# Products of the C rows and the states of a selective scan, in instructions of four states

## What is computed

```python
delta = softplus(einsum('er,brl->bel', dt_proj_w, dt_lo) + dt_proj_b)
A = -exp(A_log)                              # 512 channels x 16 states
def step(state, xs):
    d_t, B_t, C_t, u_t = xs
    dA = exp(d_t[..., None] * A)
    state = state * dA + (d_t * u_t)[..., None] * B_t[:, None, :]
    y_t = einsum('ben,bn->be', state, C_t)   # sum over the 16 states
    return state, y_t
y = (y + D * u) * silu(z)
```

## Time and profile before

| | us |
|---|---|
| median of 3 runs | 556.17 |
| lowest, highest | 554.56, 556.52 |
| the profiled execution | 554.37 |
| its span on the core | 552.6 |
| mean granted clock of PE, of full speed | 0.978 |

### The profile page before, as it was taken

How to read it: one execution, slowest core, us unless ns; L and a number is a source line. 1 busy time by engine, 2 the same in 40 slices (tenths; PEclk the granted TensorE clock), 3 DMA queues, 4 the chain that set the end, 5 groups by cost and what they waited for, 6 DMA issues and landing times.

```text
span 552.6 us, 9388 instructions
## 1 busy us (share of the span) xinstructions
PE 502.3 (91%) x3154; PEld 381.2 (69%) x3154; DVE 459.9 (83%) x844; ACT 395.3 (72%) x704; POOL 479.3 (87%) x359
## 2 busy tenths in 40 slices
PE   6668989898798899999999999999899999999788
PEld 2156979767677687759687887678667756676654
DVE  2878999969899989779899999787878878977952
ACT  3369687758776787577968787578789778777632
POOL 0169999999999999989999999989999999988920
PEclk9877999999989999999999999999999999999899
DMA  4793000127320001046220000066100000000001
GB/s 109 258 351 142 2 2 0 39 54 240 131 77 2 0 1 58 0 159 211 77 95 2 20 1 21 6 226 222 49 20 1 21 20 21 1 20 21 0 21 38
DMA packets 18274, 37.82 MB, mean 68 GB/s; under 512 B 5537, under 2 KB 6305, under 8 KB 18226
## 3 DMA queue, kind: packets, MB, share of 16 engines
q1 hardware_dynamic: 18226, 37.22, 20.3%
HBM read 32.75 MB, written 4.46 MB: 67 GB/s over the span
## 4 chain that ended last, share of the span: by engine, by line
PE 52%; POOL 15%; ACT 13%; DVE 10%; issue 8%; DMA 1%; DVEq 0%; ACTq 0%; SPq 0%; POOLq 0%
PE p_s L718 14%; PE p_y L740 12%; POOL state L541 8%; PE p_v L773 5%; PE p_f L764 5%; DVE state L1197 4%; POOL dbu L526 4%; PE p_tr L684 4%; ACT da L960 3%; PE p_pr L647 3%; DVE x L1145 2%; PE p_pr L640 2%; ACT p_s L960 2%; ACT L912 2%; ACT L960 1%
## 5 line engine op out<-in xcount | busy, mean ns | idle before, releaser
L541 POOL TENSOR_TENSOR state<-state,c_bc 128x1024 f32<-128x1024 f32 (+1 forms) x158 | 304.5, 1940 | 14.0 <-DVE state L1197 11.2
L1197 DVE TENSOR_TENSOR_SCAN state<-da,p_s 128x512 f32<-128x512 f32 (+1 forms) x158 | 172.7, 1104 | 28.7 <-PE p_s L718 27.3
L718 PEld LDWEIGHTS p_s<-pair_b,du_t 128*128 128x128 f32 x1264 | 163.9, 196 | 36.1 <-issue 22.6
L718 PE MATMUL p_s<-pair_b,du_t 128*128 128x128 f32 x1264 | 178.9, 283 | 4.0 <-DVE state L1197 2.5
L740 PE MATMUL p_y<-ident,state 128*128 128x128 f32 x1024 | 150.4, 275 | 0.8 <-POOL state L541 0.8
L960 ACT ACTIVATE da<-delta,a_neg 128x512 f32<-128x512 f32 (+1 forms) x190 | 119.2, 642 | 25.2 <-DVE state L1197 24.7
L740 PEld LDWEIGHTS p_y<-ident,state 128*128 128x128 f32 x1024 | 120.6, 142 | 20.2 <-issue 15.3
L526 POOL TENSOR_TENSOR dbu<-du,pair_b 128x1024 f32<-128x1024 f32 (+1 forms) x64 | 116.5, 1820 | 4.7 <-DMA pair_b<-bc_rows 4.7
L1197 DVE TENSOR_TENSOR_SCAN state<-p_s,dbu 128x512 f32<-128x512 f32 (+1 forms) x98 | 101.1, 1037 | 5.5 <-POOL dbu L526 4.5
L960 ACT ACTIVATE p_s<-delta,a_neg 128x512 f32<-128x512 f32 (+1 forms) x130 | 74.9, 580 | 39.4 <-DVE state L1197 38.7
L764 PE MATMUL p_f<-u_sb,h_t 128*128 128x512 f32 x112 | 55.2, 595 | 1.5 <-DVE gw L1298 1.5
(11 more groups left out here) (178 smaller groups left out, 612.9 us busy)
## 6 DMA issues: line engine op xcount, KB each, us to landing
c_bc<-bc_rows SPq DMA_DIRECT2D x32, 512.0 KB, 5.6
pair_b<-bc_rows SPq DMA_DIRECT2D x13, 512.0 KB, 6.4
xs<-in_x SPq DMA_DIRECT2D x16, 256.0 KB, 4.3
out<-ot SPq DMA_DIRECT2D x14, 256.0 KB, 2.0
cx<-in_ctx_t SPq DMA_DIRECT2D x4, 512.0 KB, 3.6
u_sb<-in_u_w SPq DMA_DIRECT2D x1, 1024.0 KB, 7.9
v_sb<-in_v_w SPq DMA_DIRECT2D x1, 1024.0 KB, 14.6
w_in<-in_in_w_t SPq DMA_DIRECT2D x1, 384.0 KB, 4.5
```

The source lines that it names most:

```text
L541: eng.tensor_tensor(pair, pair, c_bc[:, 2 * p:2 * p + 2, c0:c0 + w], ALU.mult).then_inc(po_cs, 1)
L718: mm = eng.matmul(p_s[g % BANKS][:, t * P:(t + 1) * P], du_t[:, f % 2, t, :], diagonals_of(n // 2)[:, n % 2, c0 // P + t, :], start=(t == ...
L1197: eng.tensor_tensor_scan(slot(g)[:, 0:w], decayed, added, first, ALU.mult, ALU.add).then_inc(ve_scan, 1)
```

## The change

In f = 12 to 18 POOL multiplies two pairs, four states, in one instruction, and in f = 12 to 15 copies the last columns of the four states in one. The groups are the pairs 0 and 1, 2 and 3, 4 and 5, 6 and 7; each is done at the place of its second pair and waits for the scans of all four states. The last phase and the full phases keep an instruction for each pair. Everybody who waited for a pair's product now waits for its group's.

```diff
-    C_BY_POOL = [(f, p) for f in range(F) for p in range(PAIRS) if (f, p) not in C_BY_DVE]
+    C_BY_POOL = []
+    for f in range(F):
+        if SPLIT <= f < LAST:
+            C_BY_POOL += [[(f, p), (f, p + 1)] for p in range(0, PAIRS, 2)]
+        else:
+            C_BY_POOL += [[(f, p)] for p in range(PAIRS) if (f, p) not in C_BY_DVE]
     c_by_dve = {pair: i for i, pair in enumerate(C_BY_DVE)}
-    c_by_pool = {pair: i for i, pair in enumerate(C_BY_POOL)}
+    c_by_pool = {pair: i for i, pairs in enumerate(C_BY_POOL) for pair in pairs}
...
-                g = NS * f + 2 * p
-                eng.wait_ge(ve_scan, g + 2)
+                i = c_by_pool[f, p]
+                pairs = C_BY_POOL[i]
+                if (f, p) != pairs[-1]:
+                    return
+                many = 2 * len(pairs)
+                first = 2 * pairs[0][1]
+                g = NS * f + first
+                eng.wait_ge(ve_scan, g + many)
                 if k == 0:
-                    eng.wait_ge(s_cbc[p], 16 * (b + 1))
-                pair = state[:, g % RING:g % RING + 2, 0:w]
+                    for a, q in pairs:
+                        eng.wait_ge(s_cbc[q], 16 * (b + 1))
+                states = state[:, g % RING:g % RING + many, 0:w]
                 if c0 + w < L:
-                    eng.tensor_copy(carry[:, k, 2 * p:2 * p + 2], pair[:, :, w - 1]).then_inc(po_carry, 1)
-                    eng.wait_ge(po_carry, PAIRS * (f - SPLIT) + p + 1)
-                eng.tensor_tensor(pair, pair, c_bc[:, 2 * p:2 * p + 2, c0:c0 + w], ALU.mult).then_inc(po_cs, 1)
+                    eng.tensor_copy(carry[:, k, first:first + many], states[:, :, w - 1]).then_inc(po_carry, 1)
+                    eng.wait_ge(po_carry, i - c_by_pool[SPLIT, 0] + 1)
+                eng.tensor_tensor(states, states, c_bc[:, first:first + many, c0:c0 + w], ALU.mult).then_inc(po_cs, 1)
...
-                    eng.wait_ge(po_carry, PAIRS * (f - Q - SPLIT) + n // 2 + 1)
+                    eng.wait_ge(po_carry, c_by_pool[f - Q, n // 2] - c_by_pool[SPLIT, 0] + 1)
```

## The result

Over twelve runs of each on one chip, the changed kernel takes 556.34 us (median; 554.49 to 558.18) and the kernel before 554.73 us (552.74 to 556.52): a ratio of 1.0034, 95% interval 1.0019 to 1.0049, or 1.9 us slower. That is within the half per cent called no change above, and close to the forecast of +1.75 us. The forecast time of 557.9 us is 1.6 us too high, nearly all of it because the difference was added to a median of three runs, 556.17 us, and the median of twelve lies 1.4 us lower. The profiled execution has a span of 555.3 us against 552.6, at a mean granted clock of 0.978 in both.

The account below looks back on a forecast made before the run. The prediction took PE's pace as the bound, with POOL nearly full beside it. Its terms 0.1 + 0.1 + 0.65 + 0.9 gave +1.75 us, put at 557.9 us against a median of 556.17; range 555.3 to 560.2.

Parts of the forecast that it names:

- The pace: In the half phases PE sets the pace, so about 8.5 us less POOL work brings 0 on the path.
- The price of the new form: On POOL, one product of 128 x 4 x 256 takes 2.37 us, at the other end 2.56.
- the dearer product: Rival: POOL's product of 4 x 256 costs 2.56 us, five late handovers add +1.0 us, 558.9 us; chance 0.09.
- f = 12: Pairs 4 and 5 reach PE late, against dbu coming sooner: +0.1 us, bounds -0.2 and +0.4.
- f = 16: Pairs 4 and 5 taken as in f = 12: +0.1 us, bounds -0.2 and +0.4.
- Pairs 6 and 7 of f = 13 and 14: Their group reaches PE's load of state 12 late by 0.33 us each: together +0.65 us, bounds 0 and 1.1.
- The seam: From f = 18 into the last phase, DVE's scan of state 6 waits for a later dbu: +0.9 us, bounds 0.6 and 1.2.
- The clock: Rival: in the last stretch TensorE's clock falls before PE is back, costing 1.1 us more, 559.0 us; chance 0.13.

Follow-up runs that it names:

- The kernel before with a load: Kernel before with one useless POOL product of 128 x 512 ahead of pair 3's dbu in f = 13 to 15: ratio 1.0048, stretches +2.88 us.
- the kernel with the other order: Changed kernel with the last phase's product of pair 0 behind the dbu of pair 3 instead of ahead: ratio 1.0029, stretches +1.01 us.
- filler: Four or two useless 128 x 512 products on PE in the last phase: changed kernel 1.0026 and 1.0029, kernel before 1.0026 and 1.0021.
- the early groups of the last phase: Changed kernel with pairs 0 to 3 grouped in f = 12 to 19, pairs 4 to 7 one at a time: ratio 1.0021, with filler 1.0026.

## Why the prediction was right, and where only the sum was

**The pace.** Right. The scan of state 9 of the changed kernel in f = 13 and 14:

```profile
412.24 0.69 DVE L1210 TENSOR_TENSOR_SCAN state<-da,p_s 128x256 f32<-128x256 f32 x1 [1.15 <-PE p_s L731]
...
431.12 0.69 DVE L1210 TENSOR_TENSOR_SCAN state<-da,p_s 128x256 f32<-128x256 f32 x1 [1.15 <-PE p_s L731]
```

They are 18.88 us apart, 0.21 more and not less, each still 1.15 us behind `p_s`. Seven us of POOL's work gone, and the four phases with copies gained nothing but the half us of the first. The kernel before with a load showed how near it was: some 0.1 us a phase.

**The price of the new form.** Right: 2.36 us for the forecast 2.37; the dearer product is out.

**f = 12.** The sign was wrong. The handover of pair 4 cost +0.18 for +0.1. But the `dbu` that comes sooner was set against it at 0.24 us at the most, the wait of PE for `gw` in the row at hand, and it was worth 0.50. The step that failed is that bound: it was read at the wrong place, since the wait of 1.90 us for `dbu` in this very phase was not looked for. With it in view the term is -0.3; the measured -0.32 (-0.50 and +0.18) lies outside the bounds of -0.2 to +0.4 that were given.

**f = 16.** Forecast +0.1, measured 0. "The same for f = 16" carried over the copy, which f = 16 does not have (0.27 us). PE of the changed kernel waited 0.54 us for POOL at 475.36, ahead of a product whose scan made PE wait 0.55 us before:

```profile
475.36 0.44 PE L753 MATMUL p_y<-ident,state 128*128 128x128 f32 x2 [0.54 <-POOL state L554]
```

**Pairs 6 and 7 of f = 13 and 14.** Right mechanism and place, too large: 0.22 us each for 0.33. The chain put the load at 9.89 us behind x, and it came at 9.84; of the 0.28 us by which the load was late, 0.06 were made up until the next x. Of the 0.05 us 0.04 is a slip in the sum: the group's own terms (433.35 + 0.07 + 0.27 + 2.32) leave POOL free at 436.01, where 436.05 is written. The 0.06 were not foreseen, since "without stops" was taken for "nothing to make up".

**The seam.** Right, +0.92 for +0.9, and DVE's wait is where it was forecast, if 0.77 long instead of 0.9 (its scans just before were slightly later too). The term was incomplete. What the group pushes behind the scan of state 15 also makes POOL's last products later, as the kernel with the other order showed, so mending the wait would not have mended the term.

**The clock.** Given 0.13 as a rival, and it came true: the clock fell at PE's return, and cost 0.7 to 0.8 us of the possible 1.1. The argument against it, that other work could hide part, fits the rest. Across executions of the same code the last stretch was 8.33 and 8.71 (and 7.75 to 7.99 for the code of the kernel before), so what should have been written is a term of 0.4 to 0.8 us in the sum, not a rival. Even that is for executions in which the clock falls, as it did in all three traces of the changed seam without filler; in three of the other six it did not.

The sum of the terms, +1.75, agreed with the +1.82 of the stretches and the +1.9 of the runs, because about 0.7 us too much in the phases up to f = 18 (+0.85 for +0.12) stood against 0.8 us of clock that was left out. The forecast was right on the largest term, and its closeness was in part luck.

## What to carry to other kernels

Merging instructions saves their fixed part on that engine and delays everything that the first parts had fed. Before doing so, list for each merged piece who waits for it next, and what stands behind it in the same queue; merge the early pieces of a phase, which have time, and keep the last ones of a seam apart. A longer instruction can also hold up a second engine, as the early groups of the last phase did with DVE. An engine at 95% in a window need not be the bound: look at what ends the waits of the engine whose starts repeat, and if in doubt load the suspect with a useless instruction and see whether the time grows. And where a longer wait of TensorE stands ahead of the last stretch, a delay is paid a second time if the clock falls before the work comes back.

## What the runs showed of the hardware

- POOL's fp32 product of two tensors takes 1.28 us for 512 elements a partition and 2.36 for 1024, whether in two rows or four: 0.19 to 0.20 us fixed.
- A DVE product of 128 x 512 with both inputs in SBUF takes 0.69 us alone. Where it began inside a POOL product it ended 0.55 us behind that product, each time in all traces: it took 0.84 to 1.21 us against POOL products of 1.27 us, and 1.85 against one of 2.35. A POOL product or `dbu` that stood right behind took 1.71 to 1.73 us instead of 1.27.
- A wait of TensorE of 1.94 us was followed by the fall to 1.2 GHz in six of nine traces, 0.2 to 1.1 us behind PE's return; in the other three the clock stayed up. The same code behind it took 8.71 us with the fall at 0.2 and at 0.3 us and 8.33 us with the fall at 0.7. With 1.88 or 3.60 us of useless products in that wait the clock stayed at 2.4 GHz, in all five traces.
- From execution to execution, work ahead of the half phases ended up to 4.9 us apart (378.9 to 383.7), while stretches within them that no edit touched repeated to a few hundredths of a us.
